# A transformer with gathered experts on one core: the turning of a tile's tokens moved from the start of a step to behind its first scores

## The reference

```
xn = layernorm(x)
Q, K, V = xn @ Wq.T, xn @ Wk.T, xn @ Wv.T      # 16 heads of 16 features
O = softmax(mask(Q K^T / 4)) V                 # causal, 1024 x 1024 per head
x = x + O @ Wo.T (+ bo in layer 1) + experts(xn)
```

## Time and profile before

| what | value |
|---|---|
| median of 3 runs | 3083.53 us (3082.11 to 3085.61) |
| profiled execution, span first to last instruction | 3081.5 us; what lies around it is not in the page (the fastest run is 0.6 us above the span, the median 2.0) |
| TensorE matmul busy | 2982.1 us, 97% |
| VectorE busy | 2421.1 us, 79% |
| ScalarE busy | 1972.9 us, 64% |
| GpSimd busy | 1191.8 us, 39% |
| mean granted TensorE clock | 0.993 |

### The profile page before, as it was taken

How to read it: one execution, slowest core, us unless ns; L and a number is a source line. 1 busy time by engine, 2 the same in 40 slices (tenths; PEclk the granted TensorE clock), 3 DMA queues, 4 the chain that set the end, 5 groups by cost and what they waited for, 6 DMA issues and landing times.

```text
span 3081.5 us, 62739 instructions
## 1 busy us (share of the span) xinstructions
PE 2982.1 (97%) x19312; PEld 1582.3 (51%) x19312; DVE 2421.1 (79%) x7517; ACT 1972.9 (64%) x4954; POOL 1191.8 (39%) x1424
## 2 busy tenths in 40 slices
PE   6999999999999999999999999999999999999998
PEld 3555545444565554545455555454545556544443
DVE  7777788887777878888777887878888777787884
ACT  2666666666666666666666666666666666666665
POOL 3325234252523525335252342534435243252533
PEclk8999999999999999999999999999999999999999
DMA  5766455363655645446374554635547465453642
GB/s 166 208 180 198 133 152 156 109 191 115 187 170 145 178 136 162 132 123 186 110 211 140 166 165 134 176 110 152 178 117 212 138 176 161 126 164 109 170 137 66
DMA packets 276876, 473.27 MB, mean 154 GB/s; under 512 B 52960, under 2 KB 185792, under 8 KB 274496
## 3 DMA queue, kind: packets, MB, share of 16 engines
q1 hardware_dynamic: 236928, 379.48, 40.9%
q0 software_dynamic: 29952, 81.83, 10.2%
q10 hardware_dynamic: 9664, 7.93, 0.9%
HBM read 344.19 MB, written 130.03 MB: 154 GB/s over the span
## 4 chain that ended last, share of the span: by engine, by line
PE 81%; DVE 10%; issue 4%; ACT 3%; POOL 1%; DMA 0%; ACTq 0%; DVEq 0%; POOLq 0%
PE po L1210 17%; PE pmx L1160 15%; PE pst L1147 13%; PE pst L1194 10%; PE pmx L1290 6%; PE pst L1179 5%; DVE pmx L879 4%; PE pst L1301 4%; PE pmx L1249 3%; PE pst L1168 3%; PE pmx L1228 2%; PE pst L1216 2%; DVE rmax L875 1%; ACT probs L722 1%; ACT oraw L751 1%
## 5 line engine op out<-in xcount | busy, mean ns | idle before, releaser
L722 ACT ACTIVATE probs<-pst 128x512 f32<-128x512 f32 (+3 forms) x3072 | 1401.8, 497 | 413.5 <-PE pst L1147 409.7
L621 POOL TENSOR_SCALAR_AFFINE_SELECT probs<-probs 128x512 f32<-128x512 f32 x512 | 326.7, 638 | 1464.7 <-ACT probs L722 1463.6
L875 DVE TENSOR_REDUCE rmax<-pmx 128x1 f32<-128x512 f32 x1024 | 671.1, 683 | 127.6 <-PE pmx L1160 121.0
L1147 PE MATMUL pst<-qs,k_first 98*128 98x512 bf16 (+3 forms) x2048 | 688.6, 342 | 8.7 <-ACT probs L722 4.3
L1160 PE MATMUL pmx<-k_first,qs 96*128 96x512 bf16 (+2 forms) x2048 | 668.0, 343 | 16.1 <-DVE rmax L879 5.0
L879 DVE CUSTOM_DVE_ANT_0 pmx<-pmx,mask,rmax 128x128 f32<-128x128 f32 (+3 forms) x1024 | 534.5, 555 | 162.7 <-PE pmx L1160 152.9
L1210 PE MATMUL po<-probs,v 128*32 128x512 f32 (+3 forms) x6144 | 657.5, 500 | 4.2 <-POOL probs L621 4.1
L879 DVE CUSTOM_DVE_ANT_0 pmx<-pmx,mask 128x128 f32<-128x128 f32 (+3 forms) x1024 | 483.4, 510 | 125.7 <-PE pmx L1160 124.5
L594 POOL DMA_INDIRECT xg<-xn_rows,rows_of x368 | 357.9, 973 | 95.7 <-issue 51.4
L1160 PEld LDWEIGHTS pmx<-k_first,qs 96*128 96x128 bf16 x2048 | 198.6, 98 | 348.0 <-issue 122.5
L1160 PE MATMUL pmx<-k_second,qs 96*128 96x128 bf16 (+3 forms) x1024 | 304.2, 301 | 17.5 <-DVE otok L1016 8.7
(11 more groups left out here) (143 smaller groups left out, 3626.4 us busy)
## 6 DMA issues: line engine op xcount, KB each, us to landing
wt<-w_tiles SPq DMA_DIRECT2D x161, 513.0 KB
qk_parts<-parts SPq DMA_DIRECT2D x256, 192.0 KB
y_slots<-ys SPq DMA_DIRECT2D x368, 128.0 KB
wt<-w_tiles SPq DMA_DIRECT2D x184, 256.0 KB
qs<-qk_parts SPq DMA_DIRECT2D x128, 192.0 KB
xn_rows<-xn SPq DMA_DIRECT2D x16, 1024.0 KB, 6.4
qs<-qk_parts SPq DMA_DIRECT2D x128, 128.0 KB
k_first<-qk_parts SPq DMA_DIRECT2D x64, 192.0 KB, 3.8
```

Source lines behind the costliest of these rows:

```text
L621: pool.affine_select(out=tri, in_=tri, compare_op=ALU.is_ge, fill=0.0, base=0, pattern=[[0, GH], [1, P]], channel_multiplier=-1).then_inc( ...
L722: act.activation(probs[:, u % 2, j, 0:w], ps[:, 0:w], ACT.Exp, scale=DH ** -0.5).then_inc(st_read, 1)
L875: dve.tensor_reduce(rmax0[:, col:col + 1], src, AX_X, ALU.max).then_inc(mx_read, 1)
L1147: pe.matmul(ps[:, 0:w], keys[0:SROWS, j, k % HT * P:(k % HT + 1) * P], qs[0:SROWS, set_no(q, n) % QRING, j, a:a + w], start=True, stop=Tru ...
```

## The change

The turning of a tile's tokens moves on TensorE from before round 0 to behind round 0's scores, in ScalarE's step the copy of it moves from before exponentials 0 to behind them, and the table of the banks counts the uses in the new order. Nothing is added or removed.

```diff
@@ uses
     for g in range(BEGIN, NR * NU + END - NU):
-        if tile_turned(g):
-            st["tokens", *tile_turned(g)] = len(st)
         work = maxima_at(g)
...
             if unit(g):
                 st["unit", *unit(g), j] = len(st)
+            if j == 0 and tile_turned(g):
+                st["tokens", *tile_turned(g)] = len(st)
             if j == 0 and tile_hidden(g):
@@ scalar engine
             def step(g):
+                if unit(g):
+                    exponentials(*unit(g), 0)
                 if tile_turned(g):
                     take_tokens(*tile_turned(g))
-                if unit(g):
-                    exponentials(*unit(g), 0)
                 for q, n in set_ended(g):
@@ tensor engine
                 work = maxima_at(g)
-                if tile_turned(g):
-                    turn_tokens(*tile_turned(g))
                 for j in range(GH):
...
                     if unit(g):
                         scores(*unit(g), j)
+                    if j == 0 and tile_turned(g):
+                        turn_tokens(*tile_turned(g))
                     if j == 0 and tile_hidden(g):
```

## The result

The changed kernel takes 3090.1 us in the median (3084.6 to 3095.19, 14 runs), the kernel before 3083.6 us beside it (3079.24 to 3088.03, 14 runs). The ratio is 1.0021, with a 95% interval of 1.0014 to 1.0029: slower by 6.5 us. The forecast was 3088 us, +0.14%; the size is near it.

What follows compares the result with a forecast made beforehand. TensorE was taken as the bound (busy 97%, 81% of the chain). Terms +6.7, +1.6, -1.7 and -2.3 gave +4.3 us: span 3081.5 to 3085.8, plus 2.0 for the median, 3087.8 us; 8-in-10 range 3075 to 3098.

Steps and rivals of the forecast that it cites:

- (b): Third scores wait for the first exponentials to free their bank: +0.15 us with 512 columns and narrow maxima, +0.10 with 384.
- (a): Two transposes on TensorE take 0.22 us behind the first scores instead of 0.27 behind value products; net -0.04 us per step.
- Its sum: Third scores' wait left at positions 35, 43 and layer 0's 33, 41: 48 steps at 0.14, +6.7 us.
- (c): Where first scores have 128 columns, third scores wait for a short exponential, not the tokens' copy: up to -0.17 us per step.
- the wide ones: 64 steps with 128-column scores and wide maxima: first scores' 60 ns do not cover the transposes' weight load; gain 0.
- At 39: TensorE's gain at position 39 is taken back at 40, where the projection waits for VectorE; taken at 0.
- The wide 384 positions: Positions 5, 13, 21, without those where VectorE is behind: shorter turning, 40 x -0.04 = -1.7 us.
- 19, forecast at 0: Position 19 follows turned outputs, whose copies the turning or first scores wait for either way; 0.
- 5 in layer 1: A wide 384 position, left out of the -0.04 us saving where VectorE is behind.
- other queues: price 0: VectorE, GpSimd and SyncE keep their order; first maxima come 0.27 us earlier, second about as now; price 0.
- What is swallowed: At 17, 25, 33, 41, 1, 9 waits for a finished set's copy absorb the 0.15 in layer 1; VectorE waits cover 25, 27.

Runs made afterwards that it cites:

- back3: The changed kernel with positions 13, 19 and 21 put back to the old order; 3083.92 us against 3083.67 of the kernel before, ratio 1.0002.
- a34: The changed order with three banks for maxima and four for scores and the rest; 3183.16 us against 3232.27 for the old order with those banks.
- vbase: The kernel before with the token tiles' value products two at a time at positions 12, 14, 18, 20, outside turned steps; 3088.9 us.
- vlate: vbase with the tokens at positions 13, 19 and 21 turned behind the first scores; 3087.0 us, 1.9 less than vbase.
- late3: The kernel before with only position 3 turned behind the first scores; 3085.97 us against 3083.67, ratio 1.0008.

## Why the prediction was right

The time lay in the range, the direction was the one of the forecast, and the interval of the measured change, 4.3 to 8.9 us, just reaches the 4.3 of the forecast. The wait (b) is shown, but it does not carry the direction by itself: without the losses at 13, 19 and 21, which the forecast did not have, the kernel cannot be told from before (back3). Sign and size are in part luck. Point by point:

- **(a) The turning itself** was exact: 0.22 us instead of 0.27 behind the first scores.
- **(b) The wait of the third scores** was exact where it was counted: +0.15 forecast, +0.16 measured at 35 of layer 1, with the start of the first exponentials 0.48 us behind their scores (0.47 taken). a34 shows that the bank causes it.
- **Its sum was too large**: +6.7 us for 48 steps at 0.14. Measured (8 sequences each): 35 +1.4, 43 +1.4, 33 and 41 together +0.2, that is 3.1 us. Where the tile is of layer 1 and no set takes the wait up, it costs the full +0.16 (35, 43, also 27; at 45 +0.11 for 0.10 forecast). Where the tile is of layer 0 it costs +0.02 at 35 and 43 and nothing at 33 and 41, which the sum had at 0.14. There a loss that was in the step before the change goes away: the second expert product was let go late too. Position 35 of layer 0, before:

```profile
984.19 0.38 PE L1160 MATMUL pmx<-k_second,qs 96*128 96x512 bf16 x1
984.47 1.10 PE L1194 MATMUL pst<-wt,hT 128*128 128x256 f32 x4
985.41 0.38 PE L1147 MATMUL pst<-qs,k_first 98*128 98x512 bf16 x1
```

  It stood 0.28 us behind the maxima and occupied 0.94; in the changed kernel the same step has 983.00, 983.22 and 984.08, so 0.22 and 0.86. That returns 0.14 of the 0.16. At 43 it is the same (0.29 and 0.94 before, 0.22 and 0.86 after).
- **(c) 128 columns**: right in direction. 11 gave -3.2 us instead of -2.3; 47 gave -1.8 and the wide ones about -1.4 that I had set to nothing. The reason that I gave for the wide ones, that S0's 60 ns do not cover the weight load, does not hold: at 39 and 11 the transposes behind 128-column scores take 0.22 us as well (1374.08 to 1374.30 at 39). At 39 the gain came to nothing as forecast, but not in the way forecast: not the projection of step 40 takes it back, and the fourth scores don't wait for the tokens' copy; the fourth maxima wait for VectorE in step 39 itself:

```profile
1374.67 0.23 PE L1147 MATMUL pst<-qs,k_second 98*128 98x128 bf16 x1
1374.93 0.39 PE L1160 MATMUL pmx<-k_first,qs 96*128 96x512 bf16 x1
1374.93 0.10 PEld L1160 LDWEIGHTS pmx<-k_first,qs 96*128 96x128 bf16 x1 [0.17 <-DVE rmax L879]
```

- **The wide 384 positions** were forecast at -1.7 us and are the term that failed: 13 and 21 gave +1.6 us each, and 19, forecast at 0, +3.4. I had counted that a product whose bank is free before its turn loses nothing. That is so for the scores, and the pair vbase and vlate, held against the changed kernel, shows that it is not so for a float32 product. At 19 of layer 1 about half of the +0.21 is something else: the plain wait behind 512 columns (0.11 in vlate), which I had taken as hidden by the turned outputs.
- **5 in layer 1**, +3.5 us, forecast at 0 (with +0.7 at 4 of layer 1): the step "other queues: price 0" failed, since at position 3 the turning stops the second maxima for VectorE (late3).
- **What is swallowed**: sets turned at 17, 25, 33 and 41 took up the 0.15 as said (+0.01 measured there in layer 1). At 27 of layer 1 it was not swallowed (+0.16, +1.3 us).

Together: about 4 us too much at the 512- and 384-column positions, some 13 us not counted (13, 21, 19, 5, 27), and some 4 us of gains not counted (11, 47, the wide ones). By position that makes +9.8 us, more than twice the forecast. The forecast of +4.3 came near the measured +6.5 because these errors in part offset each other, and because the time came out lower than the positions add up to. That part is luck.

The rule of the Trainium skill ("TensorE: Matmul & The Clock Gate", section "Architectural detail"), by which weight loads can be pulled ahead of matmuls in flight, holds behind scores and maxima here (transposes 0.22 us) and not behind the value products (0.27). The rows decide.

## What to carry to other kernels

When a use of a ring of buffers is moved, the distances in the ring change for its neighbours too: write down for each product whose reading it waits for, before and after, and compare that time with its turn. The same move gained 0.20 us at one position and lost 0.21 at another, so it is worth placing it by the kind of step; the position table of two profiles shows changes of 0.01 us per step that the total time cannot. It does so only if steps of one kind are grouped: the median of two kinds (+0.02 and +0.16 at position 43) is a change that no step has. And what stands behind a waiting instruction may feed an engine whose delay shows only two steps later.

## What the runs showed of the hardware

- A float32 product whose bank was let go 0.08 us before its turn started 0.06 us late and occupied 0.97 us instead of 0.89; bfloat16 scores in its place, let go 0.07 us before, lost nothing. Counted from the end of the exponentials, the float32 product started 0.14 us later at 21 (1303.85 to 1303.99) and 0.15 at 19 (1294.59 + 0.60 to 1295.34); scores that wait started 0.05 later at 35 (1362.64 to 1362.69). The load rows show that the product's first weight load waited too; that this load is what costs the 0.14 is my reading, and wasn't tested by itself.
- With TensorE idle in part before them (busy 5.36 of 7.00 us before the first), three stretches of the profile of before ran at 1.2 GHz (granted clock 0.57 over 4 us), and none in the middle of the changed kernel's, though TensorE was idle in part there too (busy 5.16 of the 6 us from 1319 to 1325). They cost about 1.6 us each, as much as the wait (b) at 10 steps.
